# Sixty-seven TensorE transposes into an unused PSUM bank, placed in the pauses of the first three batches

## The reference

```python
mod = (_silu(L0_c) @ L0_wmod).reshape(L0_c.shape[0], 6, 1, -1)
sa, ca, ga, sb, cb, gb = (mod[:, i] for i in range(6))      # ga, gb: sign kept, at least 0.25 in size
h = _layernorm(x) * (1 + ca) + sa
x = x + ga * attention(h, W, b)          # causal, one head of width 128
h = _layernorm(x) * (1 + cb) + sb
x = x + gb * routed_attention(h, ...)
```

## Time and profile before

| what | us |
|---|---|
| median of 3 runs | 486.13 (484.67 to 486.96) |
| profiled execution, whole | 486.84 |
| its span, first to last instruction | 485.0 |
| TensorE busy with matmuls | 442.1 (91% of the span), 4021 instructions |
| ScalarE / VectorE / GpSimd busy | 345.9 / 328.4 / 267.6 |
| mean granted TensorE clock | 0.989 of full speed |
| TensorE idle before its first instruction | 6.25 |

### The profile page before, as it was taken

How to read it: one execution, slowest core, us unless ns; L and a number is a source line. 1 busy time by engine, 2 the same in 40 slices (tenths; PEclk the granted TensorE clock), 3 DMA queues, 4 the chain that set the end, 5 groups by cost and what they waited for, 6 DMA issues and landing times.

```text
span 485.0 us, 11922 instructions
## 1 busy us (share of the span) xinstructions
PE 442.1 (91%) x4021; PEld 388.1 (80%) x4021; DVE 328.4 (68%) x1099; ACT 345.9 (71%) x1260; POOL 267.6 (55%) x325
## 2 busy tenths in 40 slices
PE   3775989999999999899987799999999999999994
PEld 1564778898989998797877688988888888888873
DVE  4766697777777888889779974555655545565551
ACT  2376889799798877777865777766777676667761
POOL 3136667576666887333333335644566666556555
PEclk9998999999999999989999999999999999999998
DMA  7790000001001001000000000100000011100002
GB/s 217 195 348 13 24 11 12 13 2 34 24 0 37 22 3 45 22 13 13 12 13 13 0 13 22 30 24 7 12 12 13 12 14 16 19 12 11 7 7 22
DMA packets 20107, 16.26 MB, mean 34 GB/s; under 512 B 1968, under 2 KB 18880, under 8 KB 19792
## 3 DMA queue, kind: packets, MB, share of 16 engines
q1 hardware_dynamic: 16480, 13.01, 9.0%
q0 software_dynamic: 2816, 2.10, 3.3%
q10 hardware_dynamic: 752, 0.40, 0.3%
HBM read 10.23 MB, written 5.28 MB: 32 GB/s over the span
## 4 chain that ended last, share of the span: by engine, by line
PE 65%; DVE 12%; ACT 4%; issue 4%; POOL 4%; POOLq 0%; ACTq 0%; DVEq 0%
PE bank L893 6%; PE bank L660 6%; PE bank L904 6%; PE bank L919 5%; PE bank L662 5%; PE bank L661 5%; PE bank L801 5%; PE bank L842 4%; PE bank L831 4%; PE bank L815 4%; PE bank L860 3%; ACT pr L591 3%; PE bank L932 3%; DVE cd_min L1196 2%; DVE nmx L1150 2%
## 5 line engine op out<-in xcount | busy, mean ns | idle before, releaser
L420 POOL TENSOR_TENSOR pr<-pr,rinv 128x512 f32<-128x512 f32 x64 | 66.6, 1042 | 85.1 <-DVE rinv L1156 85.1
L432 POOL TENSOR_TENSOR pr<-pr,rinv 128x512 f32<-128x512 f32 x64 | 72.7, 1156 | 63.6 <-DVE rinv L1301 63.6
L591 ACT ACTIVATE pr<-bank,nmx 128x128 f32<-128x128 f32 x256 | 90.9, 379 | 20.7 <-DVE nmx L1150 20.7
L634 ACT ACTIVATE pr<-bank,nmx 128x256 f32<-128x256 f32 x128 | 59.5, 487 | 19.3 <-DVE nmx L1295 19.3
L1295 DVE TENSOR_REDUCE nmx<-bank 128x2 f32<-128x512 f32 x64 | 41.9, 680 | 33.4 <-PE bank L893 33.4
L644 ACT ACTIVATE pt<-bank 128x512 f32<-128x512 f32 x64 | 38.2, 596 | 26.9 <-PE bank L904 26.9
L591 ACT ACTIVATION_READ_ACCUMULATOR pr<-bank,nmx 128x1 f32 x256 | 55.9, 218 | 0.0
L1150 DVE TENSOR_REDUCE nmx<-bank 128x4 f32<-128x512 f32 x64 | 42.8, 672 | 8.5 <-PE bank L801 8.5
L815 PE MATMUL bank<-ident,pr 128*128 128x128 f32 x256 | 39.0, 275 | 7.5 <-POOL pr L420 6.9
L904 PE MATMUL bank<-ident,pr 128*128 128x128 f32 x256 | 38.8, 274 | 1.6 <-ACT pt L644 1.6
L815 PEld LDWEIGHTS bank<-ident,pr 128*128 128x128 f32 x256 | 29.6, 140 | 11.0 <-POOL pr L420 8.7
(11 more groups left out here) (216 smaller groups left out, 1305.7 us busy)
## 6 DMA issues: line engine op xcount, KB each, us to landing
mod_bc<-mod_rows_scratch SPq DMA_DIRECT2D x1, 2560.0 KB, 15.1
X<-in_L_attn_x SPq DMA_DIRECT2D x4, 512.0 KB, 8.0
xh_scratch<-xhs SPq DMA_DIRECT2D x16, 128.0 KB, 2.0
out<-X SPq DMA_DIRECT2D x16, 128.0 KB, 2.6
mod_bc<-mod_rows_scratch SPq DMA_DIRECT2D x1, 1024.0 KB, 7.8
wkv_raw<-in_L_ffn_wkv_light SPq DMA_DIRECT2D x1, 512.0 KB, 6.9
mod_bc<-mod_rows_scratch SPq DMA_DIRECT2D x1, 512.0 KB, 4.6
wmod_sb<-in_L_wmod ACTq DMA_DIRECT2D x1, 384.0 KB, 5.7
```

The source lines that it names most:

```text
L420: pool.tensor_tensor(q, q, rinv[u][:, :, None].broadcast_to([P, 4, P]), ALU.mult)\
L432: pool.tensor_tensor(q, q, rinv[u][:, 0:2, None].broadcast_to([P, 2, N]), ALU.mult)\
L591: act.activation(pr[u][:, i * P:(i + 1) * P], ps[bank][:, i * P:(i + 1) * P], ACT.Exp, bias=nmx[u][:, i:i + 1], accum_out=sums[u][:, i:i + ...
L634: act.activation(pr[u][:, i * N:(i + 1) * N], ps[bank][:, i * N:(i + 1) * N], ACT.Exp, bias=nmx[u][:, i:i + 1], accum_out=sums[u][:, i:i + ...
```

## The change: what it does

TensorE gets a helper `keep_busy(n)` that transposes the identity n times into the first 128 columns of PSUM bank 0. Nothing reads these columns, and the calls carry no wait and no semaphore increment of their own.

```diff
+            def keep_busy(n):
+                for _ in range(n):
+                    pe.transpose(ps[0][:, 0:P], ident[:, :], ident[:, :])
+
             pe.wait_ge(g_tab, 1)
+            keep_busy(15)
             pe.wait_ge(c_act, 1)
             pe.transpose(ps[4][:, 0:B], c_s[:, :], ident[0:B, 0:B]).then_inc(cT_ps, 1)
+            keep_busy(6)
             pe.wait_ge(cT_sb, 1)
...
             def h_transpose(b):
+                if b in (0, 2):
+                    keep_busy(8)
                 pe.wait_ge(a["xl"], 2 * b + 2)
...
             def query_key(b):
+                if b == 0:
+                    keep_busy(6)
                 pe.wait_ge(a["hT"], b + 1)
...
             def scores_a(b):
                 k = b % 2
+                if b < 3:
+                    keep_busy(8)
                 pe.wait_ge(a["qkT"], 2 * b + 2)
```

## The result

The changed kernel takes 482.58 us (median of 11 executions, 481.24 to 483.68), the kernel before 486.13, measured beside it: ratio 0.9929, 95% interval 0.9917 to 0.9941. (The ratios are taken over the executions, so they differ a little from the ratio of two medians.) That is 3.5 us faster; 481.6 was predicted, so the gain was forecast at 4.5 to 5.0. The profiled execution took 482.58 us with a span of 480.7, 4.3 us less than before.

A forecast was written before the change was run, and what follows sets the result against it. TensorE's low clock was taken to slow the first 27 us, TensorE's pace to bound the rest; halved early steps summed to a 5.0 us shift, 481.8 from the profiled 486.84 or 481.1 from the median; predicted 481.6, range 479.8 to 487.0.

The forecast's parts named there:

- What bounds the start: First 27 us: work goes round TensorE, ScalarE and VectorE in turn, with TensorE slow at 1.2 GHz.
- Steps 1 to 7: Modulation product to heavy transposes at L688: TensorE's steps halve at the raised clock, adding up to a shift of 5.0 us.
- the wait that I had put at L688: Heavy transposes would start at 21.6 but wait for `wv_hT`, landing at 22.0; shift 5.0 in place of 5.4 us.
- Step 8: Behind L688 the clock was high before too, so the remaining work moves as a whole, by 5.0 us.
- such falls: Later clock falls, as at 40 to 44 us and 206.84, might change places: 1.5 us allowed on either side.
- Do the dummies raise the clock: Question whether transposes count towards raising TensorE's clock: 481.8 us if they do, about 491 by the Trainium skill's rule.
- the lean of the rows: TensorE's work before the rise near 27 us suggests transposes count like matmuls, giving 481.8 us.
- The slower rival: Transposes do not count; uncovered dummies cost 0.213 us each on TensorE, sum 4.4 us, 491.2 us; chance 0.12.

The follow-up runs named there:

- 34 more in the pause of 4 us: All 67 dummies plus 34 ahead of batch 4's transposes, against the kernel before: 483.19 us, ratio 0.9947.
- 21 dummies alone: Only the 21 dummies ahead of the modulation product kept, the 46 between the steps removed, against the kernel before: 485.74 us, ratio 0.9980.
- 34 misplaced: All 67 dummies plus 34 ahead of batch 3's transposes, where there is no pause, against the kernel before: 484.82 us, ratio 0.9983.
- 46 alone: Only the 46 dummies between the steps of the first batches kept, the first 21 removed, against the kernel before: 482.92 us, ratio 0.9937.
- 21 + 92: The first 21 dummies kept and the 46 between the steps doubled to 92, against the kernel before: 485.45 us, ratio 0.9977.
- the last version: 67 dummies, statistics two slots later, 44 more in early pauses, 49 in the four longest late pauses, against the kernel before: 480.13 us, ratio 0.9890.

## Why the prediction was right, and where it was not

- What bounds the start was right: the low rate of the first 27 us was the clock.
- Steps 1 to 7 were right in sum, 5.27 us measured against 5.0. `sm` of batch 0 comes 16.73 - 15.01 = 1.72 earlier (2.0 forecast), the second 3.70 (3.9), `va` 4.56 (4.65), the heavy transposes 5.27 (5.0). `mod_raw` moved by 1.67 in place of 1.08, since the conditioning vectors landed 0.5 us sooner in this execution, which is luck. With it the heavy weights' DMA moved, so the wait that I had put at L688 did not come. The sum does not hang on this luck: in the run with 34 more in the pause of 4 us the vectors were 0.17 us sooner, and the heavy transposes (L694, at 21.47) 5.54 earlier.

```profile
15.80 0.62 SPq L317 DMA_DIRECT2D wv_hT<-in_L_ffn_wkv_heavy  x1
```
```profile
DMA to landing us min/median/max: 4.9/5.2/5.4
```

The weights land at 15.80 + 5.4 = 21.2 at the latest, ahead of 21.74.
- Step 8 failed: "moves as a whole, by 5.0 us". At the 4 us pause the fall lasted about 10 us where it had lasted 3.4, and 1.8 us of shift went. I had allowed 1.5 us for such falls on either side and put the expected value at zero. The fall behind 206.84 us that did not come gave 0.8 back, so that 4.3 us were left at the end, where the sum had 5.0. That 0.8 is luck, since the later traces have from none to three late falls. The runs with 21 dummies alone and with 34 misplaced lost the same 1.8 us at that pause, to a fall of the same length; the two whose fall there was short (46 alone, 21 + 92) lost none.
- "Do the dummies raise the clock": the lean of the rows was right. By the Trainium skill ("TensorE: Matmul & The Clock Gate", Part 4: PE-mode transpose) transposes do not engage the higher clock; for these float32 transposes the runs disagree: 22 of them and nothing else stood ahead of the rise at 7.3 us. The first 21 did not do it every time: seven of the eight traces that have them show the clock up by the modulation product (L680 takes 1.03 us), the run with 92 does not (1.89).
- The slower rival did not happen in the profile of the changed kernel. Its price is real where the clock is low: 3.5 us for sixteen uncovered dummies in the run with 92.
- That the fillers between the steps hold the clock I had taken for a side matter; the run with 21 alone shows that without them the early rise is worth 0.7 us by the medians.

What stays open is why the fall at the same pause lasts 3.4 us in one execution and 10 in another. The six traces that leave the pause at 4.0 us show one difference: the three long falls (the change, 21 alone, 34 misplaced) began 0.8 to 1.1 us before the pause ended, the three short ones (the kernel before, 46 alone, 21 + 92) 0.3 to 1.0 us after TensorE had started again. What decides where a fall begins, no run shows. Nor does one show why a pause of 1.7 to 1.9 us is followed by a fall in some executions only, or why the rise of the first dummies came at 7.3 us in one trace and after 14 in another.

## What to carry to other kernels

Compare the pitch of the same small matmul early and late in the trace before trusting the granted clock's column: a start at the low level shows in the pitch, not in the column. Dummies in TensorE's pauses were free here while they ended before the awaited semaphore and cost 0.11 us each (0.22 at the low clock) when they didn't, so count them against each pause, at the rate of the clock that will be there. In two runs a fall followed the next pause once the longest was filled. What paid was the sum: filling all pauses above about 0.6 us early on and the four longest later, and taking the cause of the longest away. Which of these brought how much, the medians do not tell apart.

## What the runs showed of the hardware that was not expected

Float32 transposes alone raised the clock, near 7.3 us in the changed kernel. A raised clock fell again 0.3 us after a single pause of 1.36 us, in the run with 21 dummies. Late falls of 3.4 us cost 0.8 to 1.0 us each of the end time, and the fall of 10 us at the 4 us pause 1.8 us more than one of 3.4. How many an execution has varies: the kernel before ranged over 2.6 us, and over 2.1 beside the last version, which ranged over 1.4 and has none ahead of its last matmul in its profile.
